# Two engines instead of one for the copy of the transposed queries

## The chip, the cores and the metric

The kernel runs on one core of a Trainium2 chip. The metric is the device time of one execution in microseconds (us); the median of several executions is compared. Five engines work side by side, each through its own list of instructions in order: TensorE (PE in the profile; its weight loads are PEld), VectorE (DVE), ScalarE (ACT), GpSimd (POOL) and SyncE (SP), which here only issues DMAs. They meet through semaphores: an instruction waits until a counter has reached a value, and another engine's instruction raises that counter when it is done.

## The reference

An input of 16 sequences of 256 tokens with 128 channels goes through one small windowed attention and then through six layers, each an attention and a feed-forward part. The change lies in the attention of these six layers:

```python
def attn_layer(x, Wqkv, qs, ksc, Wo):          # HEADS = 16, DIM_HEAD = 64, WINDOW = 32
    q, k, v = split(x @ Wqkv)                    # 16 heads of 64
    q = l2norm(q) * qs
    k = l2norm(k) * ksc
    q = q * cos * scale + rotate_half(q) * sin * scale
    k = k * cos / scale + rotate_half(k) * sin / scale
    out = local_attention(q, k, v)               # each window of 32 sees itself and the one before
    return out @ Wo
for i in range(6):
    x = attn_layer(shift_tokens(x), ...) + x
    x = ffn_layer(shift_tokens(x), ...) + x
```

Everything is computed in 32-bit floating point, the projections as three products of split operands.

## The kernel before

The program has a first stage (the small attention, `stage1`), then six rounds of `prepare`, `attention` and `feed_forward`, with a meeting of all engines between them (`meet`), then `finish`.

The attention part works on 32 blocks of 128 tokens, two blocks to a sequence. `steps` (L526) runs t from 0 to 35, written out in the program, and each engine has one function for a step (`attention_pe`, `attention_act`, `attention_dve`, `attention_pool`). In step t four blocks are in flight: block t is projected, squared and rotated; block t-1 is normalised, transposed and its scores computed; block t-2 goes through the softmax; block t-3 is weighed with the values and projected out. `pl.has(k)` says whether block t-k exists. The order within a step is written out by hand in these four functions; there is no scheduler. So an instruction that waits holds up everything that stands behind it on its engine.

One step, in the words of the lines:

- **PE** (`attention_pe`): q projection of block t (six matmuls of 512 columns, recorded under L237); transposes of the probabilities of block t-3 (eight, L240); k projection; transposes of q of block t-1 (eight, L240, into the PSUM tensor `PC`; raises `qkT_done`); values times probabilities of block t-3 (128 small matmuls on a quarter of the array, L237, `PT,VB` and `PT,VA` in the profile); transposes of k of block t-1 (again into `PC`, so they wait until q has been copied out: `qkT_kept`, L592); v projection; mask and scores of block t-1; output projection of block t-3.
- **ACT** (`attention_act`): square of q (L632), copy of the transposed probabilities (L635), exp (L639), square of k (L644), two copies of the transposed q out of `PC` (L649), copy of the attention output (L654), copy of the transposed k (L659), copy of v (L666), two small steps of the reciprocal root (L670, L672), and every second step the rounding of the next sequence's input (L683, L684).
- **DVE** (`attention_dve`): row maximum of block t-2 (L716), residual add of block t-4 (L719), subtraction of the maximum (L724), rotation of q of block t (L703 and L707), sum of squares of q (L711), rotation of k (L703, L707), sum of squares of k (L711), row sums of block t-2 (L743), their reciprocal (L747).
- **POOL** (`attention_pool`): scaling of q and of k of block t-1 (L756, twice), adding up the two rotation products of q and of k of block t (L761, twice), a guard (L764), every second step the low part of the next sequence's input (L692, L694), weighing of the probabilities of block t-2 (L771), four small steps of the reciprocal root (L774 to L783), of which the last makes the factors that the next scaling waits for.

A step with odd t holds the second block of a sequence; only there ACT and POOL prepare the input of the next sequence, and the q projection of the following even step waits for it (`xs_ready`).

The transposed q of a pair of heads has the even head in partitions 0 to 63 and the odd head in 64 to 127. The target `qT` is laid out as a block-diagonal operand: for every window the even head's 32 columns stand in the upper half of the partitions and the odd head's 32 columns, one window width further, in the lower half; the rest is zero from `prepare_dve`. That is why there are two copies, one for each half of the partitions.

## Time and profile before

| | us |
|---|---|
| median of 3 runs | 4211.06 |
| lowest, highest | 4209.29, 4214.24 |
| the profiled execution | 4217.23 |
| its span from the first to the last instruction | 4215.4 |

| engine | busy us | share of the span |
|---|---|---|
| PE | 3366.9 | 80% |
| PE weight loads | 2706.9 | 64% |
| DVE | 2825.6 | 67% |
| POOL | 2464.1 | 58% |
| ACT | 2277.5 | 54% |

The profile comes from one execution. It gives the busy time of each engine, groups of instructions by line, who waited for whom, the chain of work that ended last (followed backwards from the end, at each instruction to what released it), and instructions in order of time. Times within the trace are counted from the span's start. A duration of an instruction is longer than the distance to the next one on DVE and ACT, since their ends and starts overlap by about 0.1 us: an instruction of 1.22 us on DVE is followed by the next after 1.13 us. Where an instruction is added to an engine's list, this distance is its price. "PEclk" and "granted clock" are the rate that TensorE was given, 1.00 being 2.4 GHz and 0.50 being 1.2 GHz.

### The profile page before, as it was taken

Reading aid. Unit: us, or ns where it says so; the run is one execution under the profiler, and the core shown is the slowest. Engines: PE = TensorE matmul, PEld = TensorE weight load, DVE = VectorE, ACT = ScalarE, POOL = GpSimd, SP = SyncE. Lnnn points to the kernel's source line nnn. Section 1 sums busy time; section 2 is a strip of 40 time slices with the busy share of each in tenths; the row PEclk is TensorE's granted clock in tenths of the full one; section 3 lists DMA queues with packets and bytes.
Section 4 is the critical chain, followed back from the end, with each engine's and each line's share of the span. In section 5 each row is a group of like instructions: output and inputs, shape, how many; then the busy total and the mean of one; then the engine's idle time right before and its main releaser. Section 6 shows DMA issues by size and latency. Waiting matters only on the chain.

```text
span 4215.4 us, 123316 instructions
## 1 busy us (share of the span) xinstructions
PE 3366.9 (80%) x51712; PEld 2706.9 (64%) x51904; DVE 2825.6 (67%) x4288; ACT 2277.5 (54%) x3111; POOL 2464.1 (58%) x2209
## 2 busy tenths in 40 slices
PE   3444459999769998689997799997799997699987
PEld 2323347777557777467776477775477775577774
DVE  6676767776567775577775577775577775677765
ACT  2222246666356665366664366664466663466653
POOL 0000048887168886188884288883488881688860
PEclk7666679999889999799998899998899998899997
DMA  1000001111011111011111011110011110111100
GB/s 49 0 0 0 0 23 32 34 32 34 21 33 33 34 32 44 8 32 34 37 32 36 15 32 34 32 34 31 24 32 34 32 34 22 29 37 34 32 25 20
DMA packets 37536, 117.24 MB, mean 28 GB/s; under 512 B 6144, under 2 KB 11776, under 8 KB 36224
## 3 DMA queue, kind: packets, MB, share of 16 engines
q1 hardware_dynamic: 36992, 109.44, 8.7%
q8 instruction: 408, 6.68, 0.7%
q14 instruction: 136, 1.11, 0.1%
HBM read 19.24 MB, written 2.10 MB: 5 GB/s over the span
## 4 chain that ended last, share of the span: by engine, by line
PE 38%; POOL 20%; DVE 16%; issue 15%; ACT 10%; DVEq 1%; POOLq 1%; SPq 0%; DMA 0%; PEldq 0%; ACTq 0%
PE pair L237 30%; PE pair L240 7%; POOL qk L761 6%; DVE ts L707 5%; ACT qT L649 5%; POOL qk L756 4%; POOL Sx L771 4%; DVE qk L703 3%; ACT sq L632 2%; DVE ss L711 2%; POOL xs_l L692 2%; POOL xs_l L694 1%; POOL ss L764 1%; DVE qT L382 1%; ACT PT L635 1%
## 5 line engine op out<-in xcount | busy, mean ns | idle before, releaser
L761 POOL TENSOR_TENSOR qk<-qk,ts 128x1024 f32<-128x1024 f32 x384 | 909.9, 2380 | 261.0 <-DVE ts L707 260.2
L756 POOL TENSOR_TENSOR qk<-qk,rn 128x1024 f32<-128x1024 f32 x384 | 723.8, 1906 | 15.0
L240 PE MATMUL pair<-small,qk 128*128 128x128 f32 x3384 | 505.9, 294 | 259.6 <-ACT qT L649 107.9
L703 DVE TENSOR_TENSOR qk<-pair,tab 128x1024 f32<-128x1024 f32 x384 | 468.1, 1219 | 267.3 <-ACT sq L632 267.3
L240 PEld LDWEIGHTS pair<-small,qk 128*128 128x128 f32 x3384 | 392.7, 149 | 371.5 <-issue 155.3
L237 PE MATMUL pair<-wq_h,xs_h 128*128 128x512 f32 x1152 | 516.4, 448 | 121.2 <-POOL xs_l L694 104.0
L632 ACT ACTIVATE sq<-pair 128x1024 f32<-128x1024 f32 x192 | 196.7, 1025 | 710.9 <-PE pair L237 710.9
L716 DVE TENSOR_REDUCE mx<-pair 128x16 f32<-128x1024 f32 x192 | 235.1, 1224 | 425.6 <-PE pair L237 425.6
L707 DVE TENSOR_TENSOR ts<-pair,tab 128x1024 f32<-128x1024 f32 x384 | 466.0, 1213 | 0.0
L237 PE MATMUL pair<-wq_h,xs_l 128*128 128x512 f32 x1152 | 465.1, 404 | 0.0
L237 PE MATMUL pair<-wq_l,xs_h 128*128 128x512 f32 x1152 | 464.3, 403 | 0.0
L711 DVE TENSOR_REDUCE ss<-sq 128x16 f32<-128x1024 f32 x384 | 463.8, 1208 | 0.0
L237 PEld LDWEIGHTS pair<-kT,qT 128*64 128x64 f32 x12288 | 374.9, 138 | 87.5 <-issue 87.5
L649 ACT ACTIVATE qT<-pair 64x1024 f32<-64x1024 f32 x384 | 390.6, 1017 | 46.2 <-PE pair L240 43.9
L771 POOL TENSOR_TENSOR Sx<-Sx,rden 128x1024 f32<-128x1024 f32 x192 | 365.7, 1905 | 77.1 <-DVE rden L747 70.6
L237 PE MATMUL pair<-oT,wo_sb 128*128 128x128 f32 x3072 | 398.4, 283 | 13.6 <-ACT oT L654 13.6
L237 PE MATMUL pair<-kT,qT 128*64 128x64 f32 x12288 | 401.3, 224 | 4.2 <-ACT kT L659 4.2
L237 PE MATMUL pair<-PT,VB 64*64 64x32 f32 x12288 | 378.9, 221 | 20.9 <-ACT PT L635 14.5
L237 PEld LDWEIGHTS pair<-oT,wo_sb 128*128 128x128 f32 x3072 | 361.8, 193 | 27.2 <-ACT oT L654 15.0
L237 PE MATMUL pair<-PT,VA 64*64 64x32 f32 x12288 | 375.1, 220 | 0.0
L237 PEld LDWEIGHTS pair<-PT,VB 64*64 64x64 f32 x12288 | 332.0, 135 | 54.3 <-issue 54.3
L237 PEld LDWEIGHTS pair<-PT,VA 64*64 64x64 f32 x12288 | 333.0, 136 | 0.0
(210 smaller groups left out, 5956.1 us busy)
## 6 DMA issues: line engine op xcount, KB each, us to landing
VB<-VA SPq DMA_DIRECT2D x192, 384.0 KB, 3.5
VB<-VA SPq DMA_DIRECT2D x96, 128.0 KB, 4.0
wq_raw<-wqkv SPq DMA_DIRECT2D x6, 1536.0 KB, 6.5
wo_sb<-wo SPq DMA_DIRECT2D x6, 512.0 KB, 6.7
out<-X SPq DMA_DIRECT2D x8, 256.0 KB, 2.3
w_raw<-fw SPq DMA_DIRECT2D x6, 341.0 KB, 3.1
w_sb<-fw SPq DMA_DIRECT2D x6, 192.0 KB, 3.0
qks<-qkscale SPq DMA_DIRECT2D x6, 64.0 KB, 7.0
```

What stands on the lines that cost most here:

```text
L237: return T_.matmul(out, lhsT, rhs, start=start, stop=stop, **k)
L240: return T_.transpose(out, in_, ident if idn is None else idn)
L632: A_.activation(sq[:, 0, :], one[:, :], ACT.Square).then_inc(S["squared"], 1)
L649: last = A_.activation(qT[rows, :, :, odd * WIN:(odd + 1) * WIN], PC[rows, :].rearrange("p (a w q) -> p a w q", a=PAIRS, w=4), ACT.Copy)
L692: G_.tensor_tensor(xs_l[0:64, s, :], xT[0:64, at:at + LEN], xs_h[0:64, s, :].bitcast(F32), ALU.subtract).then_inc(S["xs_ready"], 1)
L703: V_.tensor_tensor(h3(qk[:, now, kind, :], DH), h3(source[:, :], DH), rep(tab[:, 2 * kind, b, :], HEADS, DH), ALU.mult)
L707: V_.tensor_tensor(ts[:, kind, :].rearrange("p (h a c) -> p h a c", **halves), swapped, sines, ALU.mult).then_inc(S["rotated"], 1)
L711: V_.tensor_reduce(ss[:, kind * HEADS:(kind + 1) * HEADS], h3(sq[:, kind, :], DH), axis=AX.X, op=ALU.add).then_inc(S["summed"], 1)
L716: V_.tensor_reduce(mx[:, now, :], h3(PB[:, :], KEYS), axis=AX.X, op=ALU.max).then_inc(S["maxed"], 1)
L756: G_.tensor_tensor(x, x, bc(rn[:, then, kind * HEADS:(kind + 1) * HEADS], HEADS, DH), ALU.mult).then_inc(S["scaled"], 1)
L761: G_.tensor_tensor(qk[:, now, kind, :], qk[:, now, kind, :], ts[:, kind, :], ALU.add).then_inc(S["added"], 1)
L771: G_.tensor_tensor(x, x, bc(rden[:, now, :], HEADS, KEYS), ALU.mult).then_inc(S["weighed"], 1)
```

## The change

ScalarE keeps only the copy of the even heads' half (partitions 0 to 63) and raises `qkT_kept` with it. VectorE copies the odd heads' half (partitions 64 to 127) between the rotation of q and the sum of squares of q, and raises a new semaphore `odd_kept`. TensorE waits for both before it transposes k into the same PSUM tensor.

```diff
@@ attention_pe
                 e.wait_ge(S["scaled"], blocks(pl, "scaled", 1, 2))
                 e.wait_ge(S["qkT_kept"], blocks(pl, "qkT_kept", 1, 1))
+                e.wait_ge(S["odd_kept"], blocks(pl, "odd_kept", 1, 1))
                 for a in range(PAIRS):
                     last = tr(PC[:, a * P:(a + 1) * P], qk[:, then, 1, a * P:(a + 1) * P])
@@ attention_act
                 e.wait_ge(S["qkT_done"], blocks(pl, "qkT_done", 1, 1))
-                for odd in range(2):
-                    rows = slice(odd * DH, (odd + 1) * DH)
-                    last = A_.activation(qT[rows, :, :, odd * WIN:(odd + 1) * WIN],
-                                         PC[rows, :].rearrange("p (a w q) -> p a w q", a=PAIRS, w=4), ACT.Copy)
-                last.then_inc(S["qkT_kept"], 1)
+                A_.activation(qT[0:DH, :, :, 0:WIN], PC[0:DH, :].rearrange("p (a w q) -> p a w q", a=PAIRS, w=4),
+                              ACT.Copy).then_inc(S["qkT_kept"], 1)
@@ attention_dve
                     e.wait_ge(S["added"], blocks(pl, "added", 1, 1))
                 rotate(0, one)
+            if pl.has(1):
+                e.wait_ge(S["qkT_done"], blocks(pl, "qkT_done", 1, 1))
+                V_.tensor_copy(qT[DH:P, :, :, WIN:2 * WIN],
+                               PC[DH:P, :].rearrange("p (a w q) -> p a w q", a=PAIRS, w=4)).then_inc(S["odd_kept"], 1)
+            if pl.has(0):
                 if pl.has(1):
                     e.wait_ge(S["newton"], blocks(pl, "newton", 1, 1))
                 square_sums(0)
```

On DVE, in the middle of a step of the steady part, this stood before (`pair` is any of the four PSUM tensors of two banks, here the projection for L703 and L707; the names in brackets are semaphores):

```order
L703 TENSOR_TENSOR qk<-pair,tab 128x1024 [waits added,qkT_done,squared]
L707 TENSOR_TENSOR ts<-pair,tab 128x1024
L734 REGISTER_ALU
L711 TENSOR_REDUCE ss<-sq 128x16 [waits newton]
L736 REGISTER_ALU
L703 TENSOR_TENSOR qk<-pair,tab 128x1024 [waits added,squared]
L707 TENSOR_TENSOR ts<-pair,tab 128x1024
L711 TENSOR_REDUCE ss<-sq 128x16
L743 TENSOR_REDUCE den<-Sx 128x16 [waits exp_done]
L747 RECIPROCAL rden<-den 128x16 [waits rows_summed]
```

The same place with the change, where the lines of the helpers stand two lines higher:

```order
L701 TENSOR_TENSOR qk<-pair,tab 128x1024 [waits added,qkT_done,squared]
L705 TENSOR_TENSOR ts<-pair,tab 128x1024
L733 COPY qT<-pair 64x32x32 [waits qkT_done]
L737 REGISTER_ALU
L709 TENSOR_REDUCE ss<-sq 128x16 [waits newton]
L739 REGISTER_ALU
L701 TENSOR_TENSOR qk<-pair,tab 128x1024 [waits added,squared]
L705 TENSOR_TENSOR ts<-pair,tab 128x1024
L709 TENSOR_REDUCE ss<-sq 128x16
L746 TENSOR_REDUCE den<-Sx 128x16 [waits exp_done]
L750 RECIPROCAL rden<-den 128x16 [waits rows_summed]
```

One instruction came in between the two products of q and the sum of its squares, with a wait for PE; the two products of k, both sums of squares and the row sums now stand behind it.

On ACT, in the same step, this stood before:

```order
L644 ACTIVATE sq<-pair 128x1024 [waits summed]
L649 ACTIVATE qT<-pair 64x32x32 [waits qkT_done]
L649 ACTIVATE qT<-pair 64x32x32
L654 ACTIVATE oT<-pair 128x2x8x64 [waits av_done]
L659 ACTIVATE kT<-pair 128x8x128 [waits qkT_done]
```

And with the change:

```order
L645 ACTIVATE sq<-pair 128x1024 [waits summed]
L648 ACTIVATE qT<-pair 64x32x32 [waits qkT_done]
L652 ACTIVATE oT<-pair 128x2x8x64 [waits av_done]
L657 ACTIVATE kT<-pair 128x8x128 [waits qkT_done]
L664 ACTIVATE VA<-pair 128x1024 [waits vb3,av_done,v_done]
```

One of the two copies of q is gone; nothing else moved on ACT, and on PE only a wait for `odd_kept` was added to the first transpose of k.

## Rows read from the trace of the kernel before

**Rows 1.** The page's head: span and number of instructions.

```profile
span 4215.4 us, 123316 instructions
```

**Rows 2.** Page, costliest groups: count | busy us, mean ns | idle before, releaser.

```profile
L703 DVE TENSOR_TENSOR qk<-pair,tab 128x1024 f32<-128x1024 f32 x384 | 468.1, 1219 | 267.3 <-ACT sq L632 267.3
...
L649 ACT ACTIVATE qT<-pair 64x1024 f32<-64x1024 f32 x384 | 390.6, 1017 | 46.2 <-PE pair L240 43.9
```

**Rows 3.** Waits in total: waiting engine and line, releaser: us, times, longest.

```profile
PE pair L240 <- ACT qT L649: 107.9, 185, 2.5
```

**Rows 4.** The chain that ended last, four steps in layer 2: start us, us, what.

```profile
1219.33 1.04 ACT sq L632
...
1222.75 1.12 DVE ss L711
...
1225.00 1.14 DVE ts L707
...
1226.21 2.40 POOL qk L761
...
1230.42 0.72 POOL xs_l L692
...
1231.93 1.91 POOL Sx L771
...
1235.20 1.92 POOL qk L756
...
1237.16 1.11 PE pair L240 x8
...
1238.29 1.02 ACT qT L649
...
1240.49 1.06 PE pair L240 x8
...
1248.90 1.03 ACT sq L632
...
1280.37 1.03 ACT sq L632
```

**Rows 5.** PE in order of time, same steps: start, us, what, idle before.

```profile
1221.42 1.06 PE L240 MATMUL pair<-small,qk 128*128 128x128 f32 x8
...
1239.96 0.30 PE L237 MATMUL pair<-PT,VA 64*64 64x32 f32 x8
```

**Rows 6.** PE in order of time, where block t's q projection follows the output projection.

```profile
1230.04 2.05 PE L237 MATMUL pair<-oT,wo_sb 128*128 128x128 f32 x16
1231.98 0.49 PE L237 MATMUL pair<-wq_h,xs_h 128*128 128x512 f32 x1
```

**Rows 7.** DVE in order of time, same steps.

```profile
1237.08 1.21 DVE L711 TENSOR_REDUCE ss<-sq 128x16 f32<-128x1024 f32 x1
...
1245.45 1.22 DVE L716 TENSOR_REDUCE mx<-pair 128x16 f32<-128x1024 f32 x1 [2.37 <-PE pair L237]
```

**Rows 8.** POOL in order of time, same steps.

```profile
1238.93 4.72 POOL L761 TENSOR_TENSOR qk<-qk,ts 128x1024 f32<-128x1024 f32 x2
...
1247.26 3.78 POOL L756 TENSOR_TENSOR qk<-qk,rn 128x1024 f32<-128x1024 f32 x2
```

**Rows 9.** Groups of DVE instructions, shapes apart: a copy between SBUF tensors.

```profile
L831 DVE COPY qk<-xT 64x510 f32<-64x510 f32 x48 | 20.3, 423 | 0.7
```

**Rows 10.** The chain at the start of layer 1's attention, steps 1 and 2.

```profile
587.81 3.77 POOL qk L756 x2
591.57 4.63 POOL qk L761 x2
...
600.04 0.72 POOL xs_l L692
```

**Rows 11.** Windows: stretch, us, busy and count of PE, PEld, DVE, ACT, POOL, granted clock, DMA.

```profile
1255.00:1260.00 5.00, 4.93 (x51) 3.89 (x49) 3.21 (x4) 2.51 (x3) 2.65 (x2) 0.66 0.01 3
```

**Rows 12.** PE in order of time, just before that stretch.

```profile
1254.81 0.32 PE L237 MATMUL pair<-PT,VB 64*64 64x32 f32 x8 [1.23 <-issue]
```

More of the change, by code:

```diff
@@ L129, in build @@
             "seeded": 1, "newton": 3, "normed": 1, "added": 2, "scaled": 2, "qkT_done": 2, "qkT_kept": 2, "s_done": 1,
-            "maxed": 1, "shifted": 1, "exp_done": 1, "rows_summed": 1, "inverted": 1, "weighed": 1, "pT_done": 1,
+            "maxed": 1, "odd_kept": 1, "shifted": 1, "exp_done": 1, "rows_summed": 1, "inverted": 1, "weighed": 1, "pT_done": 1,
             "pT_kept": 1, "av_done": 1, "o_kept": 1, "y_done": 1, "x_updated": 1, "v_kept": 1,
```

## Prediction

> **What bounds the kernel now.** I read the page's head first [rows 1], then the waits in total, then the chain that ended last, and at last the engines in order of time for two steps that the chain shows. No engine is busy all the time (PE leads with 80% of the span), so the busy shares decide nothing. The wait at which the change aims is small: PE waits for ACT's copies of q for 107.9 us in all, 185 times, 0.58 us each [rows 3]. Even if all of it went and nothing else moved, the gain would be at most 108 us.
>
> The chain shows what a pair of steps hangs on. It repeats every 29.57 us, from one square of q to the one two steps later [rows 4]. In the odd step (it starts at 1219.33) it runs from the square of q through DVE without a break: rotation of q, sum of squares of q (1222.75), rotation of k (its second product 1225.00), then POOL adds k up (1226.21), then over the small steps to the next sequence's input (1230.42), the weighing (1231.93), the root, and the scaling of q (1235.20). From there it runs through PE: transposes of q (1237.16), both copies of q on ACT (from 1238.29), transposes of k (1240.49), and then PE alone up to the square at 1248.90. So of the two steps of a pair one is paced by DVE and POOL, the other by PE. The copies of q are on the chain in the second only.
>
> **Part 1, what ACT gives back.** One copy less, 1.03 us. In the even step both copies lie between the transposes of q and those of k, which start 3.33 us apart (1237.16 to 1240.49). But PE has other work there: the last group of the small value matmuls starts at 1239.96 [rows 5], so the transposes of k could start at about 1240.1. The gain is 0.4 us and not 1.03. The even half is copied from 1238.29 to 1239.3. In the odd step the transposes of k come earlier too, by some 0.5 us, but PE has time there: its chain is not the one that ends last, so this is worth nothing.
>
> **Part 2, what DVE pays in the odd step.** The copy goes in before the sum of squares of q, and that point is on the chain. The profile has no DVE copy out of PSUM. The nearest rows are DVE's instructions over 1024 elements per partition, of which the next starts 1.12 to 1.14 us later [rows 4]; the rotation's products read PSUM and write 1024 elements to SBUF in 1.22 us [rows 2]. I take 1.13 us. From below, DVE copies 510 elements between SBUF tensors in 0.423 us [rows 9], twice that is 0.85 us; from above 1.25 us, if the semaphore costs a tenth on top. ACT's copy of the same shape takes 1.02 us [rows 2], so the half of the partitions and the layout are no reason for a very different value.
>
> Which of the two rates holds is decided by a rule of the Trainium skill, "VectorE: DVE Perf Modes", section "Why PSUM operands drop a tier": a 32-bit operand in PSUM keeps DVE at one element a cycle, where a copy between SBUF tensors may run at two. By the cycle table in its section on the TRN2 errata the copy would take (120 + 1024) / 0.96 GHz = 1.19 us, an estimate; with the SBUF rate the pair would lose about 0.3 us less than in my sum. Another page of the Trainium skill, "PSUM — Partial Sum Buffer", section "PSUM bank collisions raise a hardware error", adds that two engines may read one bank at once if they are in different groups of 32 partitions, as they are here; no row of before shows such a pair of readers.
>
> The q transposes of this step are done at 1222.48 [rows 5], and DVE comes to the copy at about 1222.66: in the odd step the new wait costs nothing by itself. But all that follows on the chain moves by 1.13 us: rotation of k, POOL's addition, the next sequence's input, the weighing, the scaling, and with them the q projection and the transposes of q of the even step. PE does not soften it. Before, the q projection at 1231.98 followed the output projection without a pause [rows 6]; now the input lands 1.1 us later and PE waits for it.
>
> **Part 3, what DVE pays in the even step.** Before, DVE starts the sum of squares of q at 1237.08 [rows 7], while the transposes of q end at 1238.27 only [rows 4]. So DVE now stands still 1.2 us for PE and then copies for 1.13 us: the sum of squares, the rotation of k and the rest of DVE's list come 2.4 us later. Its cover: before its next row maximum DVE is idle for 2.37 us [rows 7], and PE is the pacer. DVE itself just gets through. POOL does not quite. In the time of the even step (already moved by 1.13 us as a whole), k's second product used to be done at 1237.08 + 1.13 + 1.14 + 1.22 = 1240.6 and now is at 1242.9. POOL used to add q and k in one go, 4.72 us from 1238.93 [rows 8], so k from 1241.3; now it starts on k at 1243.0, and all behind it is 1.7 us later: the weighing, the root and the next scaling, which goes from 1247.26 [rows 8] to 1249.0, with q ready after 1.9 us at 1250.9. PE wants to transpose it at 1221.42 + 29.57 - 0.4 = 1250.6 [rows 5, 4]. So the transposes, and with them DVE's copy of the odd step, come 0.1 to 0.3 us late, which is on the chain. I take 0.2 us.
>
> **Sum.** A pair: +1.13 (copy in the odd step), +0.2 (POOL late from the even step), -0.4 (PE in the even step) = +0.93 us on 29.57. A layer rotates q 384 / 2 / 6 = 32 times [rows 2], that is 31 distances or 15.5 pairs: 14.4 us. At the start of a layer it is worse. In step 1 POOL has q scaled at 587.81 + 1.9 = 589.7 and adds k up from 591.57 + 2.3 = 593.9 [rows 10]. Now k comes after the transposes (1.1 us, up to twice that at the low clock), the copy (1.13) and three more instructions of DVE (3.5): at 595.4 to 596.5, so 1.5 to 2.6 us late, and POOL's idle time before 600.04 [rows 10] may take some of it or all. Between 0 and 2.6 I take 1.5 us. A layer loses 15.9 us, six lose 95 us. The profiled execution took 4217.2 us, so 4312; it lies 6 us above the median, so the median after is forecast at 4306 us, 2.3% slower. Bounds: with 0.85 us for the copy, no POOL delay and 1 us at the start a pair loses 0.45 us and the kernel 48 us (4259); with 1.25 us, 0.3 and 2.6 us it is 1.15 us a pair and 123 us (4334).
>
> **Rivals.**
> *The relief of ACT counts and DVE's copy is hidden (faster).* DVE is idle about a third of the span, before the row maximum and before the rotation of q. If the copy fell into this idle time and only Part 1 were left, the pair would win 0.4 us and the kernel 0.4 x 93 = 37 us: 4174. It decides itself at the odd step: it needs 1.13 us of slack between the rotation of q and POOL's addition of k. The chain has none; DVE's idle time lies elsewhere. Chance 0.05.
> *Both cancel.* With a copy of 0.5 us or less gain and loss would be equal: 4211. Only a double rate out of PSUM would give it. Chance 0.03.
> *PE's clock falls (slower than forecast).* In layer 2, PE once stood still 1.23 us inside the value matmuls [rows 12], and in the next 5 us the granted clock was 0.66, so in part at 1.2 GHz instead of 2.4 [rows 11]. That pair took 31.47 us instead of 29.57 [rows 4], so stop and fall together cost 1.9 us. With the change PE stands still for about 1.6 us in every odd step before the q projection. Against it: the first pause of this kind in a layer's steady part does not recur in the profile, and the pairs after it are free of falls. If every third pair met with a fall, that is 30 x 1.9 = 57 us more: 4363. A few falls are in my range. Chance 0.12.
> *POOL's lateness from the even step becomes the bound (slower than forecast).* If k's product comes 0.5 us later than I reckon, that goes on the pair in full: 46 us more, 4352. Chance 0.08.
>
> **How the numbers follow.** Forecast 0.72, clock 0.12, POOL 0.08, hidden 0.05, cancel 0.03. The range 4262 to 4342 takes the bounds of the unknown costs, with a few clock falls at the upper end. No change that can be told is 0.2%, about 8 us: faster 0.05, same 0.03, slower 0.92.
>
> **What would show it.** Right: a pair of 30.5 us; DVE's copy at 1.2 us with the next start 1.13 us on; after the odd step's output projection a PE pause of 1 to 2 us, released by POOL's low part of the input; DVE idle about 1.2 us before the copy in the even step; the chain no longer passing through ACT's copy of q. Wrong: a copy far from 1.13 us, a pair below 29.6 us, a clock below 1.00 within the steady part, or PE waiting for the odd half before it transposes k (I expect the copy to be done 0.5 us earlier, as the value matmuls cover it).

## The result and the profile after

| | before | after |
|---|---|---|
| median, us | 4210.18 | 4370.9 |
| lowest, highest, us | 4208.56, 4214.24 | 4369.43, 4374.4 |
| span of the profiled execution, us | 4215.4 | 4367.6 |

After takes 1.0381 times as long (95%: 1.0363 to 1.0399), 161 us more. The forecast was 4306 us with 4262 to 4342 as its range: the sign was right, the size was not, and the range missed the time by 29 us. In the two profiled spans the difference is 152 us; the argument below accounts for those.

The page of after has as many instructions as that of before [rows 1]: a copy went from one engine to another.

```profile
span 4367.6 us, 123316 instructions
...
PE 3426.5 (78%) x51712; PEld 2758.7 (63%) x51904; DVE 3070.8 (70%) x4480; ACT 2078.3 (48%) x2919; POOL 2459.1 (56%) x2209
...
POOL 26%; PE 25%; issue 23%; DVE 22%; ACT 2%; DVEq 1%; POOLq 1%; SPq 0%; DMA 0%; ACTq 0%; PEldq 0%
...
L237 PE MATMUL pair<-wq_h,xs_h 128*128 128x512 f32 x1152 | 527.8, 458 | 279.8 <-POOL xs_l L692 264.6
...
L733 DVE COPY qT<-pair 64x1024 f32<-64x1024 f32 x192 | 235.8, 1228 | 155.0 <-PE pair L240 154.7
```

The last two lines are groups (count | busy us, mean ns | idle before, releaser). The new copy lasts 1.23 us where ACT's took 1.02 [rows 2]; DVE waits for PE before it for 154.7 us in all, of which the even steps have 1.13 us each (96 x 1.13 = 108, forecast 1.2) and the odd steps 0.26 (25 us); the rest lies in the first and the last step of each layer. PE now waits for POOL's low part of the input before the q projection. The line above them is the chain by engine: ACT has 2% of it.

Two steps of layer 1 on the chain that ended last (start us, us, what), to be read against [rows 4]:

```profile
882.29 1.91 POOL Sx L774
...
887.53 1.11 PE pair L240 x8
...
889.92 1.22 DVE ss L709
891.17 1.23 DVE qk L701
892.39 1.14 DVE ts L705
...
893.61 1.10 POOL qk L764
...
901.54 1.11 PE pair L240 x8
...
903.93 1.22 DVE ss L709
905.18 1.23 DVE qk L701
906.40 1.14 DVE ts L705
...
907.61 2.38 POOL qk L764
...
911.80 0.72 POOL xs_l L690
...
913.30 1.91 POOL Sx L774
```

A pair of steps takes 913.30 - 882.29 = 31.0 us, where it was 29.57 and I forecast 30.5. The second thing to see is that **both** steps now run the same way round: transposes of q, then (between the lines) DVE's copy, sum of squares, rotation of k, POOL's addition, weighing, scaling, and the next transposes of q. Of PE only the transposes of q are left on it. Before, one step of the two ran through PE.

DVE in order of time over the same steps (start, us, line, operation, idle before and its releaser):

```profile
888.66 1.23 DVE L733 COPY qT<-pair 64x1024 f32<-64x1024 f32 x1 [1.13 <-PE pair L240]
889.92 1.22 DVE L709 TENSOR_REDUCE ss<-sq 128x16 f32<-128x1024 f32 x1
891.17 1.23 DVE L701 TENSOR_TENSOR qk<-pair,tab 128x1024 f32<-128x1024 f32 x1
892.31 1.22 DVE L705 TENSOR_TENSOR ts<-pair,tab 128x1024 f32<-128x1024 f32 x1
...
902.67 1.23 DVE L733 COPY qT<-pair 64x1024 f32<-64x1024 f32 x1 [0.26 <-PE pair L240]
903.93 1.22 DVE L709 TENSOR_REDUCE ss<-sq 128x16 f32<-128x1024 f32 x1
905.18 1.23 DVE L701 TENSOR_TENSOR qk<-pair,tab 128x1024 f32<-128x1024 f32 x1
```

The starts are 1.26, 1.25 and 1.14 us apart. Only the last is the distance that I took for all of DVE's instructions. Behind the copy, the sum of squares and the product behind that begin only when the one before is over (888.66 + 1.23 = 889.89; 889.92 + 1.22 = 891.14); elsewhere each begins 0.09 us before the last has ended. I call an instruction that begins only then **held**.

The best single measure for what follows is the distance between the transposes of q of one step and the next, from PE in order of time in layer 1. "Even" is from an even step's to the odd step's, "odd" the other, which contains the next sequence's input:

| kernel | even | odd | pair |
|---|---|---|---|
| before | 13.83 | 15.74 | 29.57 |
| after | 14.01 | 17.00 | 31.01 |
| change | +0.18 | +1.26 | +1.44 |

### The profile page after: what moved, and what is told of

Its sections match the earlier page's. It is cut to its first block, busy times and chain, and to the rows that moved or that the text cites. A ratio compares the mean times of both kernels' runs of the same rounds, so it can differ in the third digit from the quotient of the medians.

```text
span 4367.6 us, 123316 instructions
## 1 busy us (share of the span) xinstructions
PE 3426.5 (78%) x51712; PEld 2758.7 (63%) x51904; DVE 3070.8 (70%) x4480; ACT 2078.3 (48%) x2919; POOL 2459.1 (56%) x2209
## 3 DMA queue, kind: packets, MB, share of 16 engines
q14 instruction: 137, 1.12, 0.1%
## 4 chain that ended last, share of the span: by engine, by line
POOL 26%; PE 25%; issue 23%; DVE 22%; ACT 2%; DVEq 1%; POOLq 1%; SPq 0%; DMA 0%; ACTq 0%; PEldq 0%
PE pair L237 17%; PE pair L240 8%; POOL qk L764 7%; POOL qk L759 7%; DVE qk L701 6%; DVE ss L709 5%; DVE ts L705 5%; POOL Sx L774 4%; POOL xs_l L690 2%; POOL xs_l L692 1%; POOL rnt L779 1%; POOL rn L786 1%; POOL rnt L777 1%; POOL ss L767 1%; DVE qT L382 1%
## 5 line engine op out<-in xcount | busy, mean ns | idle before, releaser
L701 DVE TENSOR_TENSOR qk<-pair,tab 128x1024 f32<-128x1024 f32 x384 | 470.2, 1225 | 463.7 <-ACT sq L633 457.9
L237 PE MATMUL pair<-wq_h,xs_h 128*128 128x512 f32 x1152 | 527.8, 458 | 279.8 <-POOL xs_l L692 264.6
L240 PE MATMUL pair<-small,qk 128*128 128x128 f32 x3384 | 517.8, 298 | 191.0 <-POOL qk L759 114.7
L237 PE MATMUL pair<-wq_l,xs_h 128*128 128x512 f32 x1152 | 475.8, 413 | 0.0
L237 PE MATMUL pair<-wq_h,xs_l 128*128 128x512 f32 x1152 | 475.7, 413 | 0.0
L705 DVE TENSOR_TENSOR ts<-pair,tab 128x1024 f32<-128x1024 f32 x384 | 466.5, 1215 | 0.0
L633 ACT ACTIVATE sq<-pair 128x1024 f32<-128x1024 f32 x192 | 196.6, 1024 | 525.5 <-PE pair L237 525.5
L237 PEld LDWEIGHTS pair<-wq_h,xs_h 128*128 128x128 f32 x1152 | 230.2, 200 | 335.9 <-issue 185.5
L733 DVE COPY qT<-pair 64x1024 f32<-64x1024 f32 x192 | 235.8, 1228 | 155.0 <-PE pair L240 154.7
```

What stands on the lines that cost most here:

```text
L237: return T_.matmul(out, lhsT, rhs, start=start, stop=stop, **k)
L240: return T_.transpose(out, in_, ident if idn is None else idn)
L633: A_.activation(sq[:, 0, :], one[:, :], ACT.Square).then_inc(S["squared"], 1)
L701: V_.tensor_tensor(h3(qk[:, now, kind, :], DH), h3(source[:, :], DH), rep(tab[:, 2 * kind, b, :], HEADS, DH), ALU.mult)
L705: V_.tensor_tensor(ts[:, kind, :].rearrange("p (h a c) -> p h a c", **halves), swapped, sines, ALU.mult).then_inc(S["rotated"], 1)
L733: V_.tensor_copy(qT[DH:P, :, :, WIN:2 * WIN], PC[DH:P, :].rearrange("p (a w q) -> p a w q", a=PAIRS, w=4)).then_inc(S["odd_kept"], 1)
```

## The experiments

Each ratio is to the kernel before, run on the same chip, with its 95% interval in brackets. The diffs are shortened: `...` stands for code left out, and where a kernel copies into `spare`, the line that declares this tensor is not shown. "Even" and "odd" are the distances of the table above.

### Each part of the change alone

ScalarE's part: the copy of the odd half is left out altogether.

```diff
--- after
+++ e2_scalar_part_alone
@@ attention_pe
-                e.wait_ge(S["odd_kept"], blocks(pl, "odd_kept", 1, 1))
@@ attention_dve
-            if pl.has(1):
-                e.wait_ge(S["qkT_done"], blocks(pl, "qkT_done", 1, 1))
-                V_.tensor_copy(qT[DH:P, :, :, WIN:2 * WIN], ...).then_inc(S["odd_kept"], 1)
```

> ScalarE copies the even half only and nobody copies the odd half: the odd heads' queries are left out of the scores. This is the ScalarE part of the change alone. Theory L (closed loop): 0.4 us a pair is gained in the even step, where PE can start the transposes of k only when the value matmuls are through: a pair 29.1 to 29.2 us, the kernel 4172 us (4162 to 4182). Rival F (the copies are on the path with their full 1.03 us): 4115 us. Rival N (ScalarE's copy is hidden): 4211 us.

Measured: 4169.46 us, ratio 0.9897 (0.9881 to 0.9912); even 13.55, odd 15.73. So the relief is worth 0.28 us in the even step, against 0.4 forecast, and nothing in the odd one.

VectorE's part: ACT copies both halves as before, and DVE copies partitions 64 to 127 of the q projection in PSUM, in the same place of its list, into a tensor that nobody reads.

```diff
--- after
+++ e3_vector_part_alone
@@ attention_act
-                A_.activation(qT[0:DH, :, :, 0:WIN], PC[0:DH, :] ...).then_inc(S["qkT_kept"], 1)
+                for odd in range(2):
+                    ...
+                last.then_inc(S["qkT_kept"], 1)
@@ attention_dve
-                V_.tensor_copy(qT[DH:P, :, :, WIN:2 * WIN], PC[DH:P, :] ...).then_inc(S["odd_kept"], 1)
+                V_.tensor_copy(spare[DH:P, :, :, :], one[DH:P, :] ...).then_inc(S["odd_kept"], 1)
```

> As the kernel before, ScalarE copying both halves, but VectorE in addition copies as much (64 partitions, 1024 elements, from the PSUM tensor of the q projection, upper half of the partitions) into a tensor that nobody reads, at the place and with the waits of the change. This is the VectorE part alone. Theory L (VectorE and POOL form a loop that closes in every step: transposes of q, copy, sum of squares, rotation of k, addition, weighing, root, scaling of q; PE's transposes of k are not in it, so ScalarE's relief is worth nothing any more): as the changed kernel, 31.0 us a pair and 4371 us (4362 to 4382). Rival A (the two parts add, as in the forecast): ScalarE's 0.4 us a pair is missing, 31.4 us a pair, 4408 us.

Measured: 4359.49 us, ratio 1.0345 (1.0329 to 1.0361), 2.5 us below the range of theory L and far from rival A; even 14.01, odd 16.99, to 0.01 us the distances of after. The chain of this kernel, in the same columns as before:

```profile
888.02 1.10 PE pair L241 x8
...
890.41 1.22 DVE ss L713
891.66 1.23 DVE qk L705
...
902.03 1.10 PE pair L241 x8
```

This is the loop of after (L713 and L705 are its sum of squares and first product), with ACT doing its full work. If the parts simply added up, after would be at 4359 - 42 = 4317. It is at 4371. So ACT's relief, worth 42 us alone, is worth nothing beside DVE's part: the loop passes neither ACT's copies of q nor PE's transposes of k.

### Which half DVE copies

```diff
--- after
+++ e1_halves_swapped
@@ attention_act
-                A_.activation(qT[0:DH, :, :, 0:WIN], PC[0:DH, :] ...)
+                A_.activation(qT[DH:P, :, :, WIN:2 * WIN], PC[DH:P, :] ...)
@@ attention_dve
-                V_.tensor_copy(qT[DH:P, :, :, WIN:2 * WIN], PC[DH:P, :] ...)
+                V_.tensor_copy(qT[0:DH, :, :, 0:WIN], PC[0:DH, :] ...)
```

> VectorE copies the even half (partitions 0 to 63) and ScalarE the odd half; sizes, places and waits stay as in the changed kernel. Theory H (a VectorE instruction whose operands start at another partition than those of the instruction before it starts only after that one is over: 0.13 us lost for the sum of squares behind the copy and 0.13 us for the rotation behind that, twice a pair): all instructions start at partition 0 again, the distances behind the copy go from 1.26 and 1.25 back to about 1.13 us, a pair from 31.0 to 30.5 us, the kernel to 4322 us (4310 to 4335). Rival W (the wait for PE in the middle of VectorE's list, or a copy as such, breaks the overlap): nothing changes, 4371 us.

Measured: 4323.83 us, ratio 1.026 (1.0244 to 1.0276); even 13.74, odd 16.72, pair 30.46. DVE in order of time:

```profile
897.52 1.22 DVE L733 COPY qT<-pair 64x1024 f32<-64x1024 f32 x1
898.66 1.20 DVE L709 TENSOR_REDUCE ss<-sq 128x16 f32<-128x1024 f32 x1
899.79 1.21 DVE L701 TENSOR_TENSOR qk<-pair,tab 128x1024 f32<-128x1024 f32 x1
```

The same work in the same order, and the distances are 1.14 and 1.13. The copy lasts 1.22 us, so it is hardly faster; ACT's copy, now at partition 64, still takes 1.02 us. What differs is that the partitions of DVE's copy begin at 0, as those of all its neighbours do. That is worth 0.55 us a pair and 47 us in the whole. The chain runs through PE again in the even step:

```profile
882.66 1.09 PE pair L240 x8
...
885.75 1.02 PE pair L240 x8
886.77 7.25 PE pair L237 x94
```

But it is a near tie: POOL has q scaled at 896.35 and the next transposes of q start at 896.40, when PE has just ended its k projection (896.28). At 13.74 us the loop through DVE and POOL is still longer than PE's own way of 13.55 in e2.

### The hold by itself

Two kernels add to the kernel before one tiny DVE copy behind the rotation of q; they differ in its partitions.

```diff
--- before
+++ e10_small_copy_at_64
@@ attention_dve
                 rotate(0, one)
+                V_.tensor_copy(spare[DH:P, :], tab[DH:P, 0, 0, 0:8])
```

```diff
--- before
+++ e11_small_copy_at_0
@@ attention_dve
                 rotate(0, one)
+                V_.tensor_copy(spare[0:DH, :], tab[0:DH, 0, 0, 0:8])
```

> The kernel before, with one more VectorE instruction that nobody waits for: a copy of 8 elements in partitions 64 to 127, SBUF to SBUF, behind the rotation of q in every step. Theory H: the small copy and the sum of squares behind it each wait until VectorE has run empty; in the odd step that is some 0.25 us more than the same copy at partition 0, so 0.25 x 93 = 23 us slower than e11.

> The same small copy in partitions 0 to 63. Theory H: it overlaps with its neighbours and costs its own length only, some 0.06 to 0.1 us in the odd step: 4211 + 0.08 x 93 = 4218 us (4213 to 4225), and e10 4241 us (4230 to 4255). Rival W (any further instruction costs the same, wherever it starts): e10 and e11 alike.

Measured: 4247.53 us, ratio 1.0094 (1.0077 to 1.011), odd step 16.05; and 4225.01 us, ratio 1.0038 (1.0024 to 1.0051), odd step 15.81. The first lies in the range given for it, the second at the upper edge of its own. The difference of 22.5 us over 93 pairs is 0.24 us. DVE in order of time in an odd step, first with the copy at partition 64:

```profile
891.27 1.22 DVE L708 TENSOR_TENSOR ts<-pair,tab 128x1024 f32<-128x1024 f32 x1
892.52 0.17 DVE L734 COPY spare<-tab 64x8 f32<-64x8 f32 x1
892.70 1.22 DVE L712 TENSOR_REDUCE ss<-sq 128x16 f32<-128x1024 f32 x1
893.84 1.22 DVE L704 TENSOR_TENSOR qk<-pair,tab 128x1024 f32<-128x1024 f32 x1
```

and with the copy at partition 0:

```profile
886.43 1.22 DVE L708 TENSOR_TENSOR ts<-pair,tab 128x1024 f32<-128x1024 f32 x1
887.57 0.15 DVE L734 COPY spare<-tab 64x8 f32<-64x8 f32 x1
887.63 1.20 DVE L712 TENSOR_REDUCE ss<-sq 128x16 f32<-128x1024 f32 x1
888.76 1.21 DVE L704 TENSOR_TENSOR qk<-pair,tab 128x1024 f32<-128x1024 f32 x1
```

From the product L708 to the sum of squares it is 1.43 us in the one and 1.20 in the other. At partition 64 the copy waits for the end of L708, and the sum of squares for the end of the copy; the product L704 comes 1.14 us after the sum of squares, unheld. In after that product was held too. The difference between the two copies is their source: SBUF here, PSUM there, and L704 (L701 in after) is the first to read PSUM again.

The Trainium skill has this as a rule, which I had not drawn on: "VectorE: DVE Perf Modes", section "Two Vector instructions with no wait between them". An instruction waits for all earlier ones to finish if an input starts in another group of 32 partitions than the input of the last instruction that read the same memory, or if its output starts in another group than the output of the last one that wrote there. By that rule, SBUF and PSUM being kept apart, exactly the copy, the sum of squares and the following product are held in after, and not the product here. The traces agree: the last two are seen held in after, the copy's own hold is hidden there behind its wait for PE and shows in e5 below (1.25 us), and the product here is free. The price, 0.12 us for each held one, is theirs.

### Half as long, and later

```diff
--- after
+++ e5_half_as_long
@@ attention_dve
-                V_.tensor_copy(qT[DH:P, :, :, WIN:2 * WIN], PC[DH:P, :] ...)
+                V_.tensor_copy(qT[DH:P, 0:PAIRS // 2, :, WIN:2 * WIN], PC[DH:P, 0:4 * P] ...)
```

This one copies four of the eight pairs of heads; the others are left out.

> As the changed kernel, but VectorE copies only the first four of the eight pairs of heads: half the elements, about 0.53 us less per copy; the rest of the odd half is left out. Theory L (the copy is on the closed loop in both steps of a pair, so a pair gains twice the 0.53 us until PE takes over in the even step): 29.9 to 30.1 us a pair, the kernel 4275 us (4265 to 4288). Rival S (the copy is on the chain once a pair, in the odd step, as the forecast had it): 0.53 us a pair, 30.5 us and 4322 us.

Measured: 4295.91 us, ratio 1.0202 (1.0181 to 1.0223), between the two expectations and in the range of neither; even 13.56, odd 16.71.

```profile
893.59 1.22 DVE L705 TENSOR_TENSOR ts<-pair,tab 128x1024 f32<-128x1024 f32 x1
894.84 0.70 DVE L733 COPY qT<-pair 64x512 f32<-64x512 f32 x1
895.56 1.22 DVE L709 TENSOR_REDUCE ss<-sq 128x16 f32<-128x1024 f32 x1
896.82 1.22 DVE L701 TENSOR_TENSOR qk<-pair,tab 128x1024 f32<-128x1024 f32 x1
```

The odd step pays 0.72 us for the copy, 0.12 for the copy's own hold (1.25 instead of 1.13) and 0.13 for the hold of L701: 0.97, and 16.71 - 15.74 = 0.97. The even step falls back to the 13.56 us of e2: here the loop is shorter than PE's way, and ACT's relief counts again. This is the point from which the bound changes.

```diff
--- after
+++ e6_copy_later
@@ attention_dve
                 rotate(0, one)
+            if pl.has(0):
+                if pl.has(1):
+                    e.wait_ge(S["newton"], blocks(pl, "newton", 1, 1))
+                square_sums(0)
             if pl.has(1):
                 e.wait_ge(S["qkT_done"], blocks(pl, "qkT_done", 1, 1))
                 V_.tensor_copy(qT[DH:P, :, :, WIN:2 * WIN],
                                PC[DH:P, :].rearrange("p (a w q) -> p a w q", a=PAIRS, w=4)).then_inc(S["odd_kept"], 1)
             if pl.has(0):
-                if pl.has(1):
-                    e.wait_ge(S["newton"], blocks(pl, "newton", 1, 1))
-                square_sums(0)
```

> As the changed kernel, but in both steps VectorE copies behind the sum of squares of q instead of ahead of it. Theory L: in the even step VectorE does the sum of squares while PE still transposes q, so the 1.13 us in which it stood still before the copy are gone; the even step falls back to PE's length, the odd step still pays the copy: 30.3 to 30.5 us a pair, the kernel 4304 us (4290 to 4318). Rival P (only the copy's length counts, the place does not): 4371 us.

Measured: 4324.47 us, ratio 1.0275 (1.0255 to 1.0295); even 13.56, odd 17.10. The copy 1.1 us later in the list has the transposes of q nearly ready and the even step is free of the loop. In the odd step DVE pays in full, 1.26 and one hold of the copy:

```profile
898.98 1.21 DVE L709 TENSOR_REDUCE ss<-sq 128x16 f32<-128x1024 f32 x1
900.22 1.23 DVE L737 COPY qT<-pair 64x1024 f32<-64x1024 f32 x1
901.48 1.23 DVE L701 TENSOR_TENSOR qk<-pair,tab 128x1024 f32<-128x1024 f32 x1
```

1.26 + 0.11 = 1.37, and 17.10 - 15.74 = 1.36. I had expected 4304 (up to 4318) because I left the holds out there, though this was written after they were suspected: the two holds in the odd step make 0.24 x 93 = 22 us, as much as the miss of 20.

### Does PE's clock cost anything?

From 80 us behind a layer's first rotation of q to its last one, the granted clock of after falls 27 times, each time within 1.5 us behind a pause of PE before the q projection; there are 77 such pauses of 1.85 to 1.87 us in these stretches, and one of 1.21. In the same stretches of before, e1 and e3 it doesn't fall once. (In before it falls in layers 2 and 5 at 76 and 77 us, just ahead of them.) Windows of after (stretch, us, busy and count of PE, PEld, DVE, ACT, POOL, granted clock, DMA share, GB/s), and PE in order of time at the pause ahead of them:

```profile
939.00:945.00 6.00, 4.14 (x73) 3.80 (x68) 4.56 (x6) 1.48 (x5) 4.32 (x5) 1.00 0.30 90
945.00:949.00 4.00, 3.85 (x16) 3.03 (x15) 1.70 (x2) 1.74 (x2) 3.56 (x6) 0.60 0.00 0
```

```profile
944.37 0.49 PE L237 MATMUL pair<-wq_h,xs_h 128*128 128x512 f32 x1 [1.86 <-POOL xs_l L692]
```

PE stood still 1.86 us, and then ran at 0.60 of its full rate over 4 us, so for most of them at 1.2 GHz. In e3, where the pause was 1.41 us, and in e1, where it was 1.59, nothing fell. I filled part of the pause with matmuls whose result is overwritten, six in the first kernel and two short ones in the second.

```diff
--- after
+++ e7_pause_filled
@@ attention_pe
+                if b == 0 and pl.has(1):
+                    e.wait_ge(S["rotated"], blocks(pl, "rotated", 1, 2))
+                    project(one, xs_h[:, 1 - s, P:2 * P], xs_l[:, 1 - s, P:2 * P], 0)
                 if b == 0:
                     e.wait_ge(S["xs_ready"], seqs(pl, 2, 0, 2))
```

> As the changed kernel, but in even steps PE first projects the q of the block before once more into the same PSUM tensor, as six extra matmuls of 512 columns in the pause of 1.86 us in which it waits for the next sequence's input; the right projection overwrites them. Theory C (that pause makes the granted clock fall now and then, 36 times more than in the run of VectorE's part alone, whose pause is 1.41 us): nearly no falls in the steady part, a pair stays at 31.0 us and the kernel at 4360 us (4353 to 4365). Rival D (the falls come from something else or cost nothing on the loop): 4371 us or, with the extra matmuls in the way, more.

Measured: 4401.57 us, ratio 1.0461 (1.0439 to 1.0482): not theory C, and 30 us above the 4371 of rival D, which allowed for more without saying how much. Four falls were left in the steady part and the steady pair was 31.0, but PE now stood still for "issue" (0.7 to 1.5 us at a time) inside the value matmuls, in steps 24 to 27 of nearly every layer, and pairs there took up to 34 us:

```profile
954.25 0.31 PE L237 MATMUL pair<-PT,VA 64*64 64x32 f32 x6 [1.19 <-issue]
```

So this run says nothing on the clock's price. Hence the smaller filling:

```diff
--- after
+++ e9_pause_shortened
@@ attention_pe
+                if b == 0 and pl.has(1):
+                    e.wait_ge(S["rotated"], blocks(pl, "rotated", 1, 2))
+                    for u in range(2):
+                        mm(one[:, u * UNIT:(u + 1) * UNIT], ident_bf[:, :], mask_bf[:, 0, u * UNIT:(u + 1) * UNIT])
```

> As the changed kernel, but in even steps PE does two bf16 matmuls of 512 columns (identity times mask) into the tensor of the q projection before it waits for the next sequence's input; the projection overwrites them. That takes some 0.4 us of the 1.86 us pause and adds few instructions. Theory C (the clock falls of the steady part follow the long pause and cost what the changed kernel takes more than VectorE's part alone, 11 us): no falls in the steady part, 31.0 us a pair, 4360 us (4353 to 4366). Rival D (the falls cost nothing on the loop, which runs over VectorE and POOL): 4371 us whether they are there or not.

```profile
881.11 0.50 PE L237 MATMUL pair<-wq_h,xs_h 128*128 128x512 f32 x1 [1.35 <-POOL xs_l L696]
```

Measured: 4372.42 us, ratio 1.0387 (1.0366 to 1.0407). The pause is 1.35 us, no fall is left in the steady part, and the median is no lower. Beside it the change ran once more, unaltered:

> The changed kernel once more, unaltered, on the same chip as e9 to e11, for comparison: 4371 us (4363 to 4379).

Measured: 4371.99 us, ratio 1.0375 (1.0353 to 1.0397), 25 falls. From the first rotation of q to the last, a layer takes 475.5 to 476.2 us in e9, 475.8 to 477.6 here and 477.5 to 477.8 in after; over six layers the profiled execution of e9 is 6.5 us shorter there than this one and 11.6 us shorter than after. Part of that goes with the falls: from a layer's fifth distance between transposes of q to its 30th, the distances lie above their usual length by 5.9 us in all in after and 6.0 here, by 0.7 in e9 and 1.2 in e3. So the 25 to 27 falls cost about 5 us together, 0.2 us each.

In its medians e9 doesn't show this gain, and the traces say where it went in the profiled execution. Behind the last rotation of q, up to the last residual add, a layer takes 46.6 us on average in e9, 45.8 here and 44.2 in after. How long this part takes goes with the clock. Two layers of e3 (windows as above):

```profile
1055.80:1097.00 41.20, 31.28 (x775) 27.06 (x773) 19.62 (x22) 19.34 (x21) 18.37 (x14) 1.00 0.05 15
4201.80:4252.30 50.50, 41.09 (x775) 36.23 (x773) 19.66 (x22) 19.39 (x21) 18.43 (x14) 0.75 0.04 12
```

The same program takes 41.2 us at a granted clock of 1.00 and 50.5 at 0.75; in e9 the clock there is 0.78 to 0.92.

The gap between forecast and result is 65 us, and the falls of the steady part are 5 of them: the theory that the clock explains the gap has fallen, but its price is not nothing.

### Keeping the gain without the loop

By e2 the relief is worth something in the even step alone, and by e6 a copy behind the sum of squares doesn't lengthen that step.

```diff
--- after
+++ e4_even_steps_only
@@ attention_act
+                if pl.t % 2 == 0:
+                    A_.activation(qT[0:DH, :, :, 0:WIN], PC[0:DH, :] ...).then_inc(S["qkT_kept"], 1)
+                else:
+                    for odd in (1, 0):
+                        ...
+                                      ACT.Copy).then_inc(S["odd_kept" if odd else "qkT_kept"], 1)
@@ attention_dve
                 square_sums(0)
+            if pl.has(1) and pl.t % 2 == 0:
+                e.wait_ge(S["qkT_done"], blocks(pl, "qkT_done", 1, 1))
+                V_.tensor_copy(qT[DH:P, :, :, WIN:2 * WIN], PC[DH:P, :] ...).then_inc(S["odd_kept"], 1)
```

> VectorE copies the odd half only in steps with even t and behind the sum of squares of q instead of ahead of it; in odd steps ScalarE copies both halves as before. Theory L: in the even step the transposes of q are over when VectorE is through with the sum of squares, so it does not stand still, POOL gets k only 0.6 us later and the loop through VectorE stays shorter than PE's: ScalarE's 0.4 us a pair is gained, a pair takes 29.1 to 29.2 us and the kernel 4185 us (4172 to 4195). Rival A (each VectorE copy costs its 1.2 us on the chain wherever it stands): half the loss of the change, 4290 us. Rival N: 4211 us.

Measured: 4199.96 us, ratio 0.9969 (0.9957 to 0.9981), less gain than expected and outside the range: the steady pair is 29.3, but near the start of most layers one pair took 31 to 33 us. In the odd steps ACT copies the odd half first and then the even one. The last version leaves those steps alone and gives DVE the half at partition 0:

```diff
--- after
+++ e8_even_steps_trimmed
@@ attention_act
+                if pl.t % 2 == 0 and 5 < pl.t < NBLOCKS:
+                    A_.activation(qT[DH:P, :, :, WIN:2 * WIN], PC[DH:P, :] ...).then_inc(S["qkT_kept"], 1)
+                else:
+                    ...
@@ attention_dve
                 square_sums(0)
+            if pl.has(1) and pl.t % 2 == 0 and 5 < pl.t < NBLOCKS:
+                V_.tensor_copy(qT[0:DH, :, :, 0:WIN], PC[0:DH, :] ...).then_inc(S["odd_kept"], 1)
```

> As the run with the VectorE copy in even steps only, but VectorE takes the even half (partitions 0 to 63) and only in steps 6 to 30 of a layer; in the first and the last steps ScalarE copies both halves as before. Theory: a steady pair of 29.3 us as there, and the start of a layer as in the kernel before, where that run lost up to 4 us: 4185 us (4178 to 4195). Rival: the start was not the cause, 4200 us.

Measured: 4190.36 us, ratio 0.9951 (0.9934 to 0.9968); even 13.55, odd 15.74. It beats both kernels, the one before by half a per cent. There are 13 such even steps in a layer, 78 in all: 78 x 0.28 = 22 us, of which 17 were measured. It differs from e4 in two things at once, and one of its layers still had a pair of 33 us at its start, so what the first steps alone cost in e4 was not shown.

## Why the prediction was wrong in size

In short: the term that failed is DVE's price for the copy in Part 2, 1.13 us. The runs show 1.26 us and a further 0.12 us for a held instruction behind it, in both steps, and this made the way through DVE and POOL 14.01 us in the even step, so that the gain of Part 1 was lost. Point by point, in the prediction's own steps:

**Part 1, what ACT gives back.** Forecast 0.4 us in the even step and nothing in the odd. e2 measured 0.28 and 0. But in after it is collected in no step, since PE no longer paces the even one. This term of the sum was right as a part and absent in the whole.

**Part 2, the odd step.** Forecast 1.13 us for the copy; the distance from the copy to the next start is 1.26, and one more instruction is held for 0.12 behind it. The change of the whole odd step is 1.26 us and not 1.38, since the copy starts 1.13 us after the transposes of q (902.67 against 901.54), where the sum of squares of before started 1.24 us after them. The duration of the copy (1.23 us) was near the 1.19 that I had estimated from the cycle table of the Trainium skill ("VectorE: DVE Perf Modes", section on the TRN2 errata); the rate between SBUF tensors (0.85 us) doesn't hold out of PSUM. What failed was the step from a duration to a price: "the next starts 1.12 to 1.14 us later" [rows 4] was read off neighbours that all begin at partition 0, and applied to the only one that begins at 64. This is the step that the miss rests on.

**Part 3, the even step.** DVE idle before the copy: forecast 1.2 us, measured 1.13. That POOL comes late from here was seen: by my own figures q was scaled at 1250.9, 13.74 us after the transposes at 1237.16 and 0.3 us behind PE. But the sum took 0.2 of that beside PE's full gain of 0.4, and I never wrote down that DVE and POOL, with this, are a closed way that no relief of PE shortens. In after this way takes 14.01 us, where PE's takes 13.55. e1 has it without the holds: 13.74 us, just my figure, and the pair is 30.46 us against 30.5 forecast. That this sum comes out so well is partly luck, since in e1 the even step is 0.09 us shorter than before, where I had 0.2, and the odd step 0.98 longer, where I had 1.13. e1's median of 4324 us lies in my range. So the two holds in each step, 0.24 us, are the miss, and they count twice: +0.28 us in the odd step and +0.27 in the even one from e1 to after.

**The sum.** A pair cost 1.44 us and not 0.93: 15.5 x 0.51 x 6 = 47 us of the 57 that the profiled spans are apart from the forecast (152 against 95). The other 10 lie at the ends of a layer. I had put 1.5 us a layer at its start; from the first rotation of q to the last a layer lost 21.8 us, which is 15.5 x 1.44 = 22.3 less 0.6, so the start cost nothing on balance. (In that balance stand some 0.9 us a layer of clock falls in after, and in before one pair each in layers 2 and 5 that was 1.9 us longer than the rest.) Instead 2.5 us a layer came after the last rotation of q (from 41.7 to 44.2 us up to the last residual add) and about 1 us between that and the next layer's attention, neither of which I had costed. Of the 2.5 us, 0.8 remain when the clock is 1.00 (40.4 in before, 41.2 in e3); the clock fell in this part in all six layers of after and in three of before, where it made 40.4 us into 43.0. The last 8 us are between profile and median: the profiled execution of before lay 6 us above its median, that of after 1.5 below.

**Rivals.** "Hidden" and "both cancel" needed slack on the chain or a copy under 0.5 us; neither was there. "PE's clock falls" came true as an event, about every third pair, and its price was wrong: I had taken 1.9 us from a stop and a fall in a stretch that PE bounded, and here a fall costs about 0.2 us. My argument against it didn't hold either: the stop of 1.23 us in layer 2 does recur in before, as 1.24 us in layer 5 (at 3076.97), again with a fall behind it. "POOL's lateness becomes the bound" gave 4352 if k came 0.5 us later than reckoned; that was the right mechanism, given 0.08, and the holds are what made it later (0.24 us, on both steps). A range up to that rival would still have ended 19 us short.

**What would show it.** Seen as said: the copy at 1.2 us, the pause of PE before the q projection (1.86 us, by POOL's low part), DVE's idle time, the chain without ACT's copy, and in the steady part no wait of PE for the odd half (it waited twice at the start of each layer, 1.4 to 1.9 us each). Not seen: next start at 1.13 us, pair of 30.5, clock of 1.00.

**What stays open.** e3 has the same distances as after to 0.01 us, yet was 12 us faster (4359.5 against 4371 to 4372). The falls of the steady part are some 5 us of it, and the unaltered change took 4358.3 us in the one run of e12 with a granted clock of 0.906, against 4370 to 4375 at 0.897 to 0.899; e3 had 0.909 to 0.911. But e9 took 4365 to 4379 at 0.905 to 0.909, so the clock doesn't settle it. ACT's work differs between e3 and after too, and they did not run on the same chip; no run separates these. What makes the clock fall in the part behind the last rotation of q in some layers and not in others was not tried. Nor was it tried to run e7 so that its stalls for "issue" are absent.

## What to carry to other kernels

The price of an instruction put into a list is the distance to the next start, and that depends on the neighbours: look at which partition and in which memory each operand starts, and give DVE the half that starts where its other work does. Before a wait is moved from one engine to another, close the loop: add up the way from the awaited event round through both engines to its next occurrence, in every kind of step, and compare it with the pacer's; if it is longer, relief that lies outside it is worth nothing, as ACT's was here. And a gain that exists in only some steps should be taken in those alone, as e8 does.

## What the runs showed of the hardware

- An instruction of DVE on 1024 elements that is held by a change of start partition comes 0.12 us later than its neighbours would have it (1.25 to 1.26 instead of 1.13 us). A copy out of PSUM at partition 64 among work at partition 0 costs up to three of these, one from SBUF two.
- ACT and DVE read the two partition halves of the same PSUM banks at about the same time, with no loss: both start at 888.66 in after, ACT's copy took 1.02 us and DVE's 1.23. With the halves swapped (e1) it was 1.02 and 1.22, and in e3, where DVE read another tensor, 1.02 and 1.23.
- The tiny copy of 8 elements took 0.15 us in odd steps, but in even steps from the fifth or so of a layer on it ended only when POOL's scaling did (80 times in e11, 84 in e10). In e11, DVE's line and then POOL's:

```profile
902.05 1.92 DVE L734 COPY spare<-tab 64x8 f32<-64x8 f32 x1
```

```profile
900.17 3.77 POOL L758 TENSOR_TENSOR qk<-qk,rn 128x1024 f32<-128x1024 f32 x2
```

  The copy ends at 903.97 and POOL's two instructions at 903.94; in e10 it is 909.05 and 909.03. In before, the sum of squares at 1237.08 ran its usual 1.21 us beside the scaling begun at 1235.20 [rows 4, 7]. What makes the copy from SBUF to SBUF different was not tested.
- A pause of PE of 1.86 us in front of the q projection was followed by a fall of the granted clock to 1.2 GHz in 27 of 77 cases in after and 25 of 78 in e12; with 78 pauses each of 1.35 (e9), 1.40 to 1.57 (e3) and 1.58 to 1.61 us (e1) there was none.
- The part of a layer behind the last rotation of q took 41.2 us at a granted clock of 1.00 and 50.5 us at 0.75 in one execution of one program (e3), and 40.4 at 1.00 and 43.0 at 0.92 in before.
